# Waits for landed rows ahead of two of the five gathers of a batch, in a two-layer graph network kernel

## The chip, the cores and the metric

One NeuronCore of a Trainium2 chip. The metric is the device time of one execution in microseconds (us), as the median of the runs. The engines are TensorE (PE in the profile; PEld is its weight load), VectorE (DVE), ScalarE (ACT), GpSimd (POOL) and SyncE (SP), which only starts transfers here.

## The reference

12,500 nodes with 32 features, 400,000 edges sorted by destination. Two layers, each followed by a residual add and a layer norm:

```python
x = layernorm(x + L0(x, edge_attr_2, weight, root_w, root_b, edge_index))   # spline convolution
x = layernorm(x + L1(x, edge_weight, edge_attr_3, edge_index, w1, b1, w2, b2))
# L0: basis = _basis(pseudo)                        (E, 9)
#     messages = einsum('ek,ei,kio->eo', basis, x[row], weight)
#     out = zeros.at[col].add(messages) / max(degree, 1) + x @ root_w.T + root_b
# L1: R = relu(dist @ w1 + b1) @ w2 + b2            (E, 384)
#     msg = R, spherical harmonics of rel_vec and features[src], contracted per edge to 32 values
#     out = zeros.at[dst].add(msg)
```

Both layers read one node row per edge (`x[row]`, `features[src]`): that is the gather.

## The kernel before

A *unit* is 5 x 128 = 640 edges (`G = 5`), a *batch* is 5 units (`U = 5`), and there are 125 batches (`B`). For each unit GpSimd runs `gather_unit` (L165 to L171): five indirect DMAs, each of which fetches 128 rows, one for each partition, and adds 16 to `rows_landed[u]` when they are there. In layer 0 a row is 32 floats of `x`, in layer 1 it is 96 floats of `table_dram`. Each of the five units of a batch has its own `rows` buffer and its own `rows_landed` semaphore, so GpSimd may be up to five units ahead of VectorE. The indices stand in two buffers, `idx_a` for units 0 to 2 and `idx_b` for units 3 and 4. SyncE reloads `idx_a` when the rows of units 0 to 2 have landed and `idx_b` when those of units 3 and 4 have (L324, L813); after that, in layer 0, it loads the next batch's destinations and edge attributes.

**Layer 0, the first loop (L360 to L365 on GpSimd).** Batch 0 is gathered ahead of the loop; the loop gathers batches 1 to 124. For unit `u` GpSimd waits for `spread_ready`, which VectorE sets when it has multiplied the rows of the same unit of the batch before (L472), and then gathers. VectorE's `build` (L459 to L474) makes a small `basis` in PSUM (L464), a one-hot matrix of the destinations (L467) and `spread` = basis x rows (L472). Before L464 it waits until TensorE has summed the same unit of the batch before (`summed`), since both share buffers that are five units deep. TensorE's `sum_edges` (L588 to L597) multiplies the one-hot matrix by `spread` (L595). Every batch its `fold` (L605) and `weigh` (L614) finish the messages, which VectorE adds into `acc` (L481).

**Layer 1, the second loop (L827 to L834 on GpSimd).** GpSimd waits for `prods_ready[1]`, set by VectorE's `products` (L1006, L1010) five units before, and gathers. TensorE computes `radials` (L894), three tiles and then two, each followed by a drain that signals `radial_ready` (L895). VectorE multiplies them by the gathered rows. TensorE sums over edges (L904) and turns the sum (L913). Here the ring of work buffers is three units deep (`SLOTS = 3`).

The order is the order of the code on every engine; there is no scheduler. The trace names the gathers by the helper's line L169 in both loops.

Of the kernel before, what the change touches and what calls it, by code (L numbers as in the profile page):

```python
# [27 lines left out]
G = 5  # L28
# [11 lines left out]
EPS = 1e-5  # L40
SLOTS = 3
CREDIT = U


SLOT = [u % SLOTS for u in range(U)]
# [13 lines left out]
def done(g, u):  # L59

    return g * U + (u + 1)


def freed(g, u):

    return g * U + (u - AGO[u] + 1 + CREDIT)


def last_round(g, u):

    return g * U + (u - U + 1 + CREDIT)

# [54 lines left out]
def load_passes(eng, keep):  # L127

    return eng.value_load(keep["span_i"][0:1, 0:1], min_val=0, max_val=N - 1) // WINDOW + 1
# [35 lines left out]
def gather_unit(pool, table, idx, rows, width, u, gathers_begun, rows_landed):  # L165

    pool.sem_inc(gathers_begun, 1)
    for j in range(G):
        pool.indirect_dma_start(out=rows[u][:, j, 0:width], out_offset=None, in_=table,  # L169
                                in_offset=bass.IndirectOffsetOnAxis(ap=idx[u // 3][:, u % 3, j:j + 1], axis=0)  # L170
                                ).then_inc(rows_landed[u], 16)  # L171
# [28 lines left out]
def spline_layer(nc, keep, x, src, dst, edge_attr_2, edge_attr_3, weight0, root_w, root_b, spans_dram, table_dram):  # L200
# [13 lines left out]
    with ExitStack() as ctx:  # L214
# [9 lines left out]
        def sem(name):  # L224
            return ctx.enter_context(nc.semaphore(name))
# [36 lines left out]
        x_ps, root_ps = [pair[:, n, :] for n in range(2)], [msg_ps, side_ps]  # L262
        fold_ps = [bank[:, 0:3 * n * WINDOW].rearrange("k (c w) -> k c w", c=3)
                   for bank, (_, n) in zip((pair[:, 0, :], pair[:, 1, :], side_ps), FOLDS)]
        agg_ps = [pair, sums_all]
        window_ps = own_ps[:, 0:WINDOW]
# [10 lines left out]
        rows_landed = [sem(f"l0_rows_landed{n}") for n in range(U)]  # L277
# [67 lines left out]
        @block.gpsimd  # L345
        def _(pool):
            pool.memset(ident[:, :], 0.0).then_inc(ident_made, 1)
            pool.wait_ge(ident_made, 1)
            pool.affine_select(out=ident[:, :], in_=ident[:, :], compare_op=ALU.not_equal, fill=1.0, base=0,
                               pattern=[[-1, P]], channel_multiplier=1).then_inc(ident_made, 1)  # L350
            pool.iota(keep["iota"][:, :], [[1, WINDOW]], base=0, channel_multiplier=0,
                      allow_small_or_imprecise_dtypes=True).then_inc(ident_made, 1)

            for u in range(U):
                if u in (0, 3):
                    pool.wait_ge(idx_landed[u // 3], 16)
                gather_unit(pool, x, idx, rows, C, u, gathers_begun, rows_landed)
            pool.wait_ge(span_ready, 1)
            passes = load_passes(pool, keep)
            with pool.Fori(0, passes * B - 1) as g:  # L360
                for u in range(U):
                    pool.wait_ge(spread_ready, done(g, u))
                    if u in (0, 3):
                        pool.wait_ge(idx_landed[u // 3], g * 16 + 32)
                    gather_unit(pool, x, idx, rows, C, u, gathers_begun, rows_landed)  # L365

        @block.vector
        def _(dve):
# [107 lines left out]
            def add(g, u, offset):  # L476

                dve.wait_ge(msg_ready, g + 2)
                dve.wait_ge(added, g * U + (u + CREDIT))
                at = acc[0:C + 1, bass.ds(offset, WINDOW)]  # L480
                dve.tensor_tensor(at, at, msg_ps[0:C + 1, u * WINDOW:(u + 1) * WINDOW], ALU.add).then_inc(added, 1)  # L481

            dve.sem_inc(summed, CREDIT)
            dve.sem_inc(msg_ready, 1)
            dve.sem_inc(added, CREDIT)
            LAG = 2
# [68 lines left out]
        def _(pe):  # L555
# [42 lines left out]
            def fold(g, k):  # L598
                u0, n = FOLDS[k]
                pe.wait_ge(flat_ready, done(g, u0 + n - 1) + CREDIT)  # L600
                pe.wait_ge(sums_ready, g * KF + (k + 1))
# [127 lines left out]
def tensor_edges(nc, keep, src, table_dram, edge_weight, w1, b1, w2, b2):  # L729
# [9 lines left out]
    with ExitStack() as ctx:  # L739
# [9 lines left out]
        def sem(name):  # L749
            return ctx.enter_context(nc.semaphore(name))  # L750
# [22 lines left out]
        rows_landed = [sem(f"l1_rows_landed{n}") for n in range(U)]  # L773
# [20 lines left out]
        @block.sync  # L794
        def _(sp):
            for h in range(2):
                sp.sem_inc(idx_landed[h], 16)
            for h in range(2):
                load_dist(sp, 0, h)
            sp.dma_start(w2raw[0:HID, :], w2).then_inc(w_landed, 16)  # L800
            sp.dma_start(w2raw[HID:HID + 1, :], b2.rearrange("(o r) -> o r", o=1)).then_inc(w_landed, 16)
            for h in range(2):
                sp.dma_start(w1c[HID * h:HID * (h + 1), :], w1.rearrange("o h -> h o")).then_inc(w_landed, 16)
                sp.dma_start(b1c[HID * h:HID * (h + 1), :], b1.rearrange("(h o) -> h o", o=1)).then_inc(w_landed, 16)
            passes = load_passes(sp, keep)

            with sp.Fori(0, passes) as p:

                def body(i, after):
                    g = p * B + i  # L810
                    for h, (u0, u1) in enumerate(DIST):
                        for u in range(u0, u1):
                            sp.wait_ge(rows_landed[u], (g + 1) * (16 * G))  # L813
                        load_indices(sp, src, idx, idx_landed, h, after)

                with sp.Fori(0, B - 1) as i:
                    body(i, i + 1)
                body(B - 1, 0)
            for h in range(2):
                sp.wait_ge(idx_landed[h], passes * (B * 16) + 16)  # L820
            sp.sem_inc(indices_done, 1)

        @block.gpsimd
        def _(pool):
            pool.sem_inc(prods_ready[1], CREDIT)
            passes = load_passes(pool, keep)
            with pool.Fori(0, passes) as p:  # L827
                with pool.Fori(0, B) as i:
                    g = p * B + i
                    for u in range(U):  # L830
                        pool.wait_ge(prods_ready[1], g * U + (u - U + 1 + CREDIT))
                        if u in (0, 3):
                            pool.wait_ge(idx_landed[u // 3], (g + 1) * 16)
                        gather_unit(pool, table_dram, idx, rows, ROW, u, gathers_begun, rows_landed)  # L834
# [358 lines left out]
```

## Time and profile before

| | us |
|---|---|
| median of 3 runs | 10573.09 (10558.03 to 10587.41) |
| span of the profiled execution | 10807.3 |
| first loop with its start, from the timeline | 0 to 4790 |
| second loop | 4867 to 10737 |

| engine | busy us | share of the span |
|---|---|---|
| PE | 6974.1 | 65% |
| POOL | 5918.5 | 55% |
| DVE | 5904.1 | 55% |
| ACT | 2697.5 | 25% |

The page has no figure for what lies around the span; the profiled execution's own time is known here as its span, 234 us above the median of the runs. A busy share is a mean over two loops that have different limits, so each loop is read by itself. In an idle time, "issue" as releaser says that nothing in the profile ended it, and "remote" that a semaphore of another engine did which the profile can't tie to one instruction.

### The profile page before, as it was taken

The numbers are of one execution on the slowest core, as the hardware profiler recorded it, in microseconds if no ns is written. First come the engines' busy times: TensorE is split into PE (matmuls) and PEld (weight loads), VectorE is DVE, ScalarE is ACT, GpSimd is POOL, SyncE is SP. The second block draws the span as 40 slices with busy tenths as digits, with TensorE's granted clock in tenths as the row PEclk, the third lists the DMA queues.
The fourth block names the chain that finished last, engine by engine and source line by source line (L and its number), as shares of the span: only waits on it lengthen the run. The fifth ranks groups of instructions, "written<-read, shape, count | busy, mean of one in ns | idle before, by whom it ended". The sixth has DMA issues, their size and how long they took to land. (4 is left out here: it accounts for less than half of the span.)

```text
span 10807.3 us, 123454 instructions
## 1 busy us (share of the span) xinstructions
PE 6974.1 (65%) x30415; PEld 3523.6 (33%) x30415; DVE 5904.1 (55%) x14948; ACT 2697.5 (25%) x6811; POOL 5918.5 (55%) x6257
## 2 busy tenths in 40 slices
PE   5555555555554555556777777777777777777777
PEld 2222222222222222233333333333333333333334
DVE  4333433333333333346666666666666666666667
ACT  1000000000000000013333333333333333333333
POOL 6666666666666666645545554554554555455553
PEclk7666666666666666668888888888888888888888
DMA  1111111111111111112222222222222222222221
GB/s 27 13 13 13 13 13 13 13 13 13 13 13 13 13 13 13 13 27 46 45 43 43 45 45 43 43 45 43 45 43 44 43 43 45 44 44 43 44 45 42
DMA packets 640189, 331.75 MB, mean 31 GB/s; under 512 B 522098, under 2 KB 572413, under 8 KB 639919
## 3 DMA queue, kind: packets, MB, share of 16 engines
q0 software_dynamic: 200000, 205.20, 10.9%
q10 hardware_dynamic: 20000, 102.42, 3.6%
q1 hardware_dynamic: 420168, 23.91, 2.7%
q8 instruction: 8, 0.13, 0.0%
q14 instruction: 13, 0.10, 0.0%
HBM read 324.65 MB, written 6.40 MB: 31 GB/s over the span
## 5 line engine op out<-in xcount | busy, mean ns | idle before, releaser
L595 PE MATMUL sums_all<-shared 128*64 128x289 f32 x6250 | 2028.7, 500 | 2060.9 <-issue 2038.6
L169 POOL DMA_INDIRECT rows<-table_dram,idx_a x1875 | 1776.4, 947 | 1781.0 <-DVE prods L1010 1184.1
L169 POOL DMA_INDIRECT rows<-in_x,idx_a x1875 | 1774.7, 946 | 1450.6 <-DVE shared L472 910.9
L894 PE MATMUL radial_y<-w2p,hidden 128*128 128x384 f32 x2500 | 1226.5, 623 | 1209.0 <-issue 1176.1
L904 PE MATMUL sums_ps<-prods,hot 128*64 128x272 f32 x12500 | 1711.8, 423 | 256.7 <-issue 251.1
L595 PEld LDWEIGHTS sums_all<-shared 128*64 128x64 f32 x6250 | 878.1, 162 | 2988.8 <-issue 2693.5
L169 POOL DMA_INDIRECT rows<-table_dram,idx_b x1250 | 1184.0, 947 | 1204.9 <-DVE prods L1010 842.9
L464 DVE TENSOR_TENSOR own_ps<-factors 128x45 f32<-128x45 f32 x625 | 133.0, 213 | 2645.9 <-remote 2041.0
L864 ACT ACTIVATE hot<-window,rel_t 128x64 f32<-128x64 f32 x3125 | 813.2, 335 | 2487.4 <-PE sums_ps L904 1578.2
L894 PE MATMUL radial_x<-w2p,hidden 128*128 128x384 f32 x3750 | 1378.7, 504 | 34.7 <-issue 34.7
L169 POOL DMA_INDIRECT rows<-in_x,idx_b x1250 | 1182.6, 946 | 381.2 <-issue 380.9
L904 PEld LDWEIGHTS sums_ps<-prods,hot 128*64 128x64 f32 x12500 | 1007.8, 148 | 1142.9 <-issue 842.9
L682 ACT ACTIVATE flat<-sums_all 64x289 f32<-64x289 f32 x625 | 255.2, 408 | 4317.4 <-remote 3176.2
L894 PEld LDWEIGHTS radial_y<-w2p,hidden 128*128 128x128 f32 x2500 | 516.2, 229 | 1820.4 <-issue 1704.2
L1006 DVE TENSOR_TENSOR prods<-radial_x,rows 128x768 f32<-128x768 f32 x625 | 598.5, 958 | 863.2 <-PEq L895 572.5
L472 DVE TENSOR_TENSOR shared<-own_ps,rows 128x1440 f32<-128x1440 f32 x625 | 1030.0, 1648 | 12.2 <-DVE own_ps L464 10.0
L859 ACT ACTIVATE hidden<-dist_ab,b1c,w1c 64x640 f32<-64x640 f32 x625 | 959.4, 1535 | 8.6 <-issue 2.2
L1010 DVE TENSOR_TENSOR prods<-radial_x,rows 128x384 f32<-128x384 f32 x1875 | 923.0, 548 | 0.0
L894 PEld LDWEIGHTS radial_x<-w2p,hidden 128*128 128x128 f32 x3750 | 661.7, 189 | 425.4 <-issue 37.5
L1034 DVE TENSOR_REDUCE red<-sums_ps 128x16 f32<-128x272 f32 x625 | 273.6, 438 | 729.2 <-remote 565.4
L1010 DVE TENSOR_TENSOR prods<-radial_y,rows 128x384 f32<-128x384 f32 x1250 | 632.2, 547 | 0.0
L1019 DVE TENSOR_REDUCE along<-prods 128x40 f32<-128x640 f32 x625 | 506.8, 811 | 0.1
(149 smaller groups left out, 4735.0 us busy)
## 6 DMA issues: line engine op xcount, KB each, us to landing
dist_ab<-in_edge_weight ACTq DMA_DIRECT2D x125, 480.0 KB
dist_ab<-in_edge_weight ACTq DMA_DIRECT2D x125, 320.0 KB
rows<-in_x,idx_a POOLq DMA_INDIRECT x1875
rows<-table_dram,idx_a POOLq DMA_INDIRECT x1875
rows<-in_x,idx_b POOLq DMA_INDIRECT x1250
rows<-table_dram,idx_b POOLq DMA_INDIRECT x1250
vec_s<-in_edge_attr SPq DMA_DIRECT2D x126, 37.5 KB
idx_a<-in_src SPq DMA_DIRECT2D x251, 7.5 KB
```

The source lines that it names most:

```text
L169: pool.indirect_dma_start(out=rows[u][:, j, 0:width], out_offset=None, in_=table, in_offset=bass.IndirectOffsetOnAxis(ap=idx[u // 3][:, u ...
L472: dve.tensor_tensor(spread[s][:, :, 0:K].rearrange("e t (k c) -> e t k c", c=C), basis[s].unsqueeze(3).to_broadcast([P, G, 9, C]), rows[u] ...
L595: last = pe.matmul(sums_ps[s][:, 0:K + 1], hot[s][:, j, :], spread[s][:, j, :], start=(j == 0), stop=(j == G - 1))
L682: act.activation(flat[u][:, :], sums_ps[u][:, 0:K + 1], ACT.Copy).then_inc(flat_ready, 1)
L859: act.activation(hidden[s][0:HID, :].rearrange("h (j p) -> h j p", p=P), dist[u].rearrange("h (p j) -> h j p", j=G), ACT.Relu, bias=b1c[HI ...
L864: last = act.activation(hot[s][:, j, :], keep["window"][:, :], ACT.Abs, bias=rel_t[:, bass.ds(i * (U * G) + (u * G + j), 1)], scale=-1.0)
L894: pe.matmul(radial[h][:, j, 0:R], hidden[s][:, (j0 + j) * P:(j0 + j + 1) * P], w2p[:, :], start=True, stop=True)
L904: last = pe.matmul(sums_ps[s][k * WINDOW:(k + 1) * WINDOW, 0:HALF], hot[s][:, j, :], prods[s][:, j, MUL + 16 * k:MUL + 16 * (k + 1), :].re ...
L1006: dve.tensor_tensor(prods[s][:, j0:j0 + tiles, 0:16, 0:16], ra, comp[:, :, 0:1, :].to_broadcast([P, tiles, 16, 16]), ALU.mult)
L1010: last = dve.tensor_tensor(prods[s][:, j0 + j, 16:OUTS, 0:16].rearrange("e (u o) i -> e u o i", o=3), rb, comp[:, j, 1:4, :].unsqueeze(1). ...
L1019: dve.tensor_reduce(along[:, :, :], prods[SLOT[u]][:, :, 0:MUL, 0:16], AX_X, ALU.add).then_inc(along_ready, 1)
L1034: dve.tensor_reduce(red[s][:, 0:16], sums_ps[s][:, 0:HALF].rearrange("w (o i) -> w o i", i=I17), AX_X, ALU.add).then_inc(red_ready, 1)
```

## The change

`REST = (1, 3)`. In both loops GpSimd, ahead of the gathers of units 1 and 3, waits until all five gathers of the unit before (0 or 2) of the same batch have landed. Nothing is removed, and no instruction changes its place.

```diff
@@ constants
 CREDIT = U
+REST = (1, 3)
@@ first loop, GpSimd
                 for u in range(U):
                     pool.wait_ge(spread_ready, done(g, u))
+                    if u in REST:
+                        pool.wait_ge(rows_landed[u - 1], g * (16 * G) + 32 * G)
                     if u in (0, 3):
                         pool.wait_ge(idx_landed[u // 3], g * 16 + 32)
@@ second loop, GpSimd
                     for u in range(U):
                         pool.wait_ge(prods_ready[1], g * U + (u - U + 1 + CREDIT))
+                        if u in REST:
+                            pool.wait_ge(rows_landed[u - 1], (g + 1) * (16 * G))
                         if u in (0, 3):
                             pool.wait_ge(idx_landed[u // 3], (g + 1) * 16)
```

GpSimd's instructions in the body of the first loop, units 0 to 4, before:

```order
L169 DMA rows<-in_x,idx_a 128x32 [waits l0_idx_a_landed]
L169 DMA rows<-in_x,idx_a 128x32 x4
L362 REGISTER_ALU
L169 DMA rows<-in_x,idx_a 128x32 [waits spread_ready]
L169 DMA rows<-in_x,idx_a 128x32 x4
L362 REGISTER_ALU
L169 DMA rows<-in_x,idx_a 128x32 [waits spread_ready]
L169 DMA rows<-in_x,idx_a 128x32 x4
L362 REGISTER_ALU
L169 DMA rows<-in_x,idx_b 128x32 [waits spread_ready,l0_idx_b_landed]
```

and now (every line is one lower down):

```order
L170 DMA rows<-in_x,idx_a 128x32 [waits l0_idx_a_landed]
L170 DMA rows<-in_x,idx_a 128x32 x4
L363 REGISTER_ALU
L365 ISA [waits spread_ready]
L170 DMA rows<-in_x,idx_a 128x32 [waits l0_rows_landed0]
L170 DMA rows<-in_x,idx_a 128x32 x4
L363 REGISTER_ALU
L170 DMA rows<-in_x,idx_a 128x32 [waits spread_ready]
L170 DMA rows<-in_x,idx_a 128x32 x4
L363 REGISTER_ALU
L170 DMA rows<-in_x,idx_b 128x32 [waits l0_idx_b_landed,spread_ready,l0_rows_landed2]
```

The first gather of unit 1 waits for `l0_rows_landed0` and the first of unit 3 for `l0_rows_landed2` as well; what stood beside it has become one more small instruction (ISA). The second loop changes in the same way, with `l1_rows_landed0` and `l1_rows_landed2`.

## Rows read from the trace of the kernel before

**Rows 1.** The page, fifth part: two groups (busy, mean ns, idle before, releaser).
```profile
L169 POOL DMA_INDIRECT rows<-in_x,idx_a x1875 | 1774.7, 946 | 1450.6 <-DVE shared L472 910.9
...
L464 DVE TENSOR_TENSOR own_ps<-factors 128x45 f32<-128x45 f32 x625 | 133.0, 213 | 2645.9 <-remote 2041.0
```

**Rows 2.** Busy time in the two loops: us, busy (x instructions), TensorE clock, DMA, GB/s.
```profile
0.00:4790.00 4790.00, 2480.10 (x8841) 1187.46 (x8841) 1844.87 (x4743) 424.49 (x1122) 2957.47 (x3132) 0.68 0.13 14
4867.00:10737.00 5870.00, 4391.97 (x21086) 2260.56 (x21086) 3964.05 (x9956) 2227.65 (x5593) 2960.36 (x3125) 0.88 0.21 44
```

**Rows 3.** Timeline, GpSimd, layer 0: start, us, instruction, [idle before <-releaser].
```profile
2015.35 0.95 POOL L169 DMA_INDIRECT rows<-in_x,idx_a  x1 [0.30 <-issue]
2016.61 0.95 POOL L169 DMA_INDIRECT rows<-in_x,idx_b  x1 [0.30 <-issue]
...
2027.86 0.95 POOL L169 DMA_INDIRECT rows<-in_x,idx_b  x1 [0.30 <-issue]
2036.24 0.95 POOL L169 DMA_INDIRECT rows<-in_x,idx_a  x1 [7.43 <-DVE shared L472]
```

**Rows 4.** Timeline, VectorE, the same batch.
```profile
2006.45 1.65 DVE L472 TENSOR_TENSOR shared<-own_ps,rows 128x1440 f32<-128x1440 f32 x1
...
2012.12 0.45 DVE L439 TENSOR_SCALAR factors<-factors 128x50 f32<-128x50 f32 x1 [0.48 <-DVE factors L438]
2033.16 0.21 DVE L464 TENSOR_TENSOR own_ps<-factors 128x45 f32<-128x45 f32 x1 [20.59 <-remote]
...
2033.69 1.65 DVE L472 TENSOR_TENSOR shared<-own_ps,rows 128x1440 f32<-128x1440 f32 x1
```

**Rows 5.** Timeline, TensorE, the same batch.
```profile
2003.88 4.17 PE L595 MATMUL sums_all<-shared 128*64 128x289 f32 x20
...
2024.00 0.64 PE L595 MATMUL sums_all<-shared 128*64 128x289 f32 x1 [2.85 <-issue]
...
2033.45 6.41 PE L595 MATMUL sums_all<-shared 128*64 128x289 f32 x20
```

**Rows 6.** One tile, the load of idx_a: count, duration, first to last start.
```profile
L162 SPq MOVE idx_a<-in_src x1: 29/29/29, 2017.9 to 2017.9; - x1
```

**Rows 7.** One tile, the load of idx_b.
```profile
L162 SPq MOVE idx_b<-in_src x1: 29/29/29, 2030.3 to 2030.3; - x1
```

**Rows 8.** Timeline, GpSimd, an early batch with two pauses.
```profile
269.69 0.95 POOL L169 DMA_INDIRECT rows<-in_x,idx_b  x1 [0.30 <-issue]
273.09 0.95 POOL L169 DMA_INDIRECT rows<-in_x,idx_a  x1 [2.46 <-DVE shared L472]
```

**Rows 9.** Timeline, VectorE, the same early batch.
```profile
281.36 0.21 DVE L464 TENSOR_TENSOR own_ps<-factors 128x45 f32<-128x45 f32 x1 [8.71 <-remote]
```

**Rows 10.** Timeline, GpSimd, layer 1.
```profile
6369.93 0.94 POOL L169 DMA_INDIRECT rows<-table_dram,idx_a  x1 [0.30 <-issue]
6378.09 0.94 POOL L169 DMA_INDIRECT rows<-table_dram,idx_a  x1 [7.21 <-DVE prods L1010]
...
6386.26 0.95 POOL L169 DMA_INDIRECT rows<-table_dram,idx_a  x1 [2.23 <-DVE prods L1010]
...
6393.11 0.95 POOL L169 DMA_INDIRECT rows<-table_dram,idx_b  x1 [0.89 <-issue]
...
6398.11 0.94 POOL L169 DMA_INDIRECT rows<-table_dram,idx_b  x1 [0.30 <-issue]
```

**Rows 11.** Timeline, TensorE, the same stretch of layer 1.
```profile
6372.57 2.92 PE L894 MATMUL radial_y<-w2p,hidden 128*128 128x384 f32 x4 [6.32 <-issue]
...
6381.04 1.55 PE L894 MATMUL radial_y<-w2p,hidden 128*128 128x384 f32 x4
...
6387.86 1.55 PE L894 MATMUL radial_y<-w2p,hidden 128*128 128x384 f32 x4
...
6400.76 2.92 PE L894 MATMUL radial_y<-w2p,hidden 128*128 128x384 f32 x4 [6.14 <-issue]
```

**Rows 12.** Groups of instructions, TensorE, from 4870 to 10730 us.
```profile
L894 PE MATMUL radial_y<-w2p,hidden 128*128 128x384 f32 x2480 | 1218.8, 624 | 1208.6 <-issue 1176.1
```

## The prediction

> **What bounds the kernel now.** I read the mean times of the two loops first, then the timeline of one batch on GpSimd, VectorE and TensorE, then layer 1 in the same way. The first loop takes 4790 us, the second 5870 us, and in neither is an engine full: in the first GpSimd is busy for 2957 us, TensorE for 2480 us, VectorE for 1845 us [rows 2]. So look for what each waits for.
>
> Layer 0. GpSimd issues a gather every 1.25 us (0.95 busy, 0.30 to the next), 25 in a row without a gap: at 2015.35, across the unit boundary at 2016.61, up to 2027.86; then it is idle for 7.43 us, until VectorE's L472 [rows 3]. A batch is therefore 24 x 1.25 + 0.95 + 7.43 = 38.4 us, and all of those pauses are 910.9 us [rows 1]. VectorE for its part stood idle for 20.59 us, from 2012.57 to 2033.16, ahead of L464, the first instruction of a unit; such waits make up most of 2646 us [rows 1, 4]. L464 waits for TensorE's sum of the same unit one batch earlier. TensorE had done 20 matmuls from 2003.88 to 2008.05, two units, at full pace. After that it crawls: at 2024.00 one matmul after 2.85 us in which the profile shows no releaser; at 2033.45 it is suddenly at full pace again [rows 5]. It is not the arithmetic that is late. While GpSimd gathers without a break, signals and issue of TensorE are held up, and they come through when the gathers have drained: GpSimd's last gather ended at 2028.81, VectorE went on at 2033.16 (4.35 us later). VectorE then does L464 to L472, and GpSimd starts 0.90 us after L472's end (2035.34 to 2036.24) [rows 3, 4]. That is a ring: gathers without a break hold up TensorE, TensorE holds up VectorE, VectorE holds up the next batch's gathers.
>
> Layer 1 shows the same thing more sharply. TensorE stops for 6.32 us and resumes at 6372.57; GpSimd's last gather ended at 6370.87, 1.70 us before. It stops for 6.14 us and resumes at 6400.76; the gather ended at 6399.05, 1.71 us before [rows 10, 11]. Both stops fall on a unit gathered hard behind another: ahead of 6393.11 GpSimd was idle for only 0.89 us, whereas the unit at 6386.26, behind a pause of 2.23 us, stopped nobody [rows 10]. From one stop's end to the next is 28.19 us for three units, where a unit without a stop takes 6.82 us (6381.04 to 6387.86): a stop costs 28.19 - 3 x 6.82 = 7.7 us [rows 11]. In all TensorE loses 1176 us this way [rows 12], some 185 stops of 6.3 us, about three in two batches.
>
> **The change part by part.** It adds waits only. Their price first. The rows of the last gather of unit 2 (issued at 2015.35, ended at 2016.30) had landed by 2017.9, when SyncE, which waits for the same semaphore, went on; those of unit 4 ended at 2028.81 and were there by 2030.3 [rows 3, 6, 7]. So a gather's landing is signalled at most 1.5 to 1.6 us after its end. Behind a signal GpSimd needs 0.90 us to its first gather (above). A rest is 1.5 + 0.9 = 2.4 us of idle GpSimd in place of 0.3, so 2.1 us more. Bounds: below, zero, where GpSimd was idle for over 2.4 us anyway; above, 4.35 us of release plus 0.9, 5.0 us more, if the landing signal were held up as TensorE's are.
>
> Behind the waiting instruction stand, on GpSimd, only the gathers of the same and later units. Unit 1's and 2's rows come 2.1 us later, unit 3's and 4's 4.2 us, and with them SyncE's index and stream loads. VectorE consumes rows a batch after the wait for their buffer, so this is covered as long as it is behind GpSimd.
>
> Layer 0, the benefit. The first rest comes 6.25 us into a batch, at a time (2036.24 - 38.4 + 6.25 = 2004.1 in the batch shown) when TensorE still runs at full pace, and a run is then at most three units (3, 4 and the next 0) instead of five. TensorE's sums reach VectorE in the rest or at the latest in the next one, one batch before they are needed. GpSimd then never waits for VectorE and the loop goes at GpSimd's own pace: 25 x 1.25 + 2 x 2.1 = 35.5 us a batch instead of 38.4. Over the 124 batches of the loop: 911 us of pauses go, 37 us of plain 0.30 us gaps take their place, 248 rests of 2.1 us add 521 us. Net: **-353 us**. What is late next is GpSimd itself, with nothing behind it that could fill in.
>
> The Trainium skill, "DMA: Bandwidth & Descriptors", section "Rules for kernel authors", speaks against the change: issue a DMA early and wait on its semaphore late, so that its fixed cost overlaps. Its section on the anatomy of a gpsimd DMA puts that cost at about 2.0 us, near what the row gives. By that rule alone 498 rests would be an added 1.0 ms with nothing in return; the trace's 911 us of pauses, released by VectorE, is what the rule does not see.
>
> Layer 1. GpSimd's own work with rests is 25 x 1.25 + 3 x 0.6 + 2 x 2.1, about 37 us of a batch of 47, so the rests cost nothing on the path: its rows are needed four units later. They can forbid a stop at units 1 and 3, since the pause before those is then 2.4 us. But a stop forbidden at unit 3 likely moves to unit 4, which is gathered hard behind it. Now a stop comes every three units, sometimes four (185 in 625: 3.4 on average). If only 0, 2 and 4 can be hit, the cycle is 0, 4, 2, 0: steps of four, three and three. That is 3.3 to 3.6 on average, between no gain and 11 stops fewer (-85 us). I take **-50 us**. Bounds: -1170 us if the stops all went and GpSimd's 37.7 us set the pace (125 x 9.4), and +60 us.
>
> Sum: -403 us against the span of 10807 us. The median of the runs is 0.978 of that span, so I take 0.978 x 403 = 394 us from it: 10573 - 394 = **10180 us**.
>
> **Rivals.**
>
> A, slower: the rests are too short to let TensorE's signals through in layer 0. For it: there the release came 4.35 us after the last gather, and a rest is 2.4 us; in an early batch GpSimd paused for 2.46 us, from 270.64 to 273.09, and VectorE still waited until 281.36, that is until 2.3 us after the next pause began [rows 8, 9]. Against it: those followed runs of 20 to 25 gathers, while in layer 1 runs of ten released within 1.7 us, and the first rest follows five. If it holds, the pause of 7.4 us stays and 4.2 us are added to each batch: +521 us, 0.978 x 521 = 510, **11083 us**. It decides from the point at which the release needs more than 2.4 us after runs of 10 to 15 gathers. Chance 0.17, half of it a mild form near 10700.
>
> B, much faster: in layer 1 the rests break the pattern, and half of the stops or more are gone. For it: the stops follow short pauses, and two of the five are made long. Against it: GpSimd then lags and gathers units 2, 4 and 0 back to back. Half of 185 stops at 7.7 us is 712 us more: **about 9480 us**; a quarter gives 9830. Chance 0.13.
>
> C, a part: in layer 0 a pause of about 3 us remains at the end of most batches, because the run of units 3, 4 and 0 lasts 18.75 us and holds up VectorE's unit 0. That takes 3 x 124 = 372 us back: **about 10545 us**. Chance 0.12.
>
> D, the waits do nothing: they are met whenever GpSimd reaches them. The gathers at 2015.35 and 2016.61 are 0.30 us apart and the rows of the first came over 1 us later [rows 3, 6], so in layer 0 this can't be. By the skill's rule, same page, section "Issuing engines are not separate DMA queues", transfers of all engines interleave on the same 16 DMA engines. That rule gives a rest nothing to free, and its result is that of A.
>
> **How the numbers follow.** Forecast 0.58, A 0.17, B 0.13, C 0.12. The forecast's own range is 10080 to 10300: the release time of a rest between 1.9 and 2.7 us is 60 us either way, layer 1 another 50. For 8 in 10 the range reaches into C and A's mild form above and into B's weak form below: 9950 to 10620. A measurement of this kernel tells a change from none at about 0.3%, 32 us. Faster: the forecast, B and most of C, less a little for what I haven't seen, 0.77. Same: the edge of C, 0.05. Slower: A and a rest, 0.18.
>
> **What would show it.** In the changed profile the gather at the start of units 1 and 3 of layer 0 has about 2.4 us of idle time ahead of it, released by a DMA, and the one of unit 0 has 0.3 us in place of 7.4. The idle time released by L472 falls from 911 us to near zero, VectorE's waits of 20 us ahead of L464 are gone, and it waits for landed rows ahead of L472 instead. TensorE's crawl no longer fills half of a batch. GpSimd's batch takes 35.5 us in layer 0, and in layer 1 about 46.7 us, with the stops of TensorE on units 0, 2 and 4 alone. The prediction is wrong if the pause of 7 us is still there beside the rests (A), if the rest's idle time is well over 2.4 us, or if layer 1's 1176 us fall by hundreds.

## The result and the profile after

The changed kernel takes **10590.14 us** (median of 20 runs, 10566.73 to 10615.96), the kernel before in the same comparison 10570.44 us (20 runs, 10551.22 to 10592.28): ratio 1.002, 95% interval 1.0012 to 1.0029. I had forecast 10180. The change is no gain but a loss of 0.2%, small and clear of noise. In the traces alone it looks otherwise: the span went from 10807.3 to 10614.2 us.

Busy time in the two loops of the changed kernel, with the columns of [rows 2]:

```profile
0.00:4664.00 4664.00, 2689.24 (x8850) 1259.03 (x8851) 1856.22 (x4746) 421.07 (x1124) 2950.26 (x3132) 0.68 0.12 14
4738.00:10535.00 5797.00, 4336.20 (x21058) 2231.06 (x21058) 3962.17 (x9945) 2232.74 (x5593) 2952.71 (x3125) 0.88 0.20 44
```

Layer 0 is 126 us shorter than in the trace of before, layer 1 is 73 us shorter. What GpSimd and VectorE waited for in layer 0 of the changed kernel, from 100 to 4600 us (in total, times, longest), first GpSimd:

```profile
POOL rows L170 <- issue: 1157.6, 2849, 2.8
POOL rows L170 <- DVE shared L475: 332.4, 72, 6.2
POOL rows L170 <- DMA rows<-in_x,idx_a: 166.9, 94, 2.3
```

and VectorE:

```profile
DVE own_ps L467 <- remote: 1614.6, 192, 19.2
DVE own_ps L467 <- PE sums_all L598: 335.3, 77, 12.2
DVE shared L475 <- DMA rows<-in_x,idx_b: 197.5, 47, 6.1
```

GpSimd's pauses until VectorE fell from 911 us [rows 1] to 341 over the whole loop (332 in the stretch above) and did not vanish. VectorE still stands ahead of L467 (L464 before) for 1615 us, in more and shorter waits; in the same stretch of the kernel before it was:

```profile
DVE own_ps L464 <- remote: 1917.4, 116, 21.7
```

GpSimd's timeline shows the new rests, here ahead of units 1 and 3 (for most of them the profile names no releaser but "issue"), and between them a pause that should be gone:

```profile
2436.52 0.94 POOL L170 DMA_INDIRECT rows<-in_x,idx_a  x1 [2.25 <-issue]
...
2447.44 0.94 POOL L170 DMA_INDIRECT rows<-in_x,idx_a  x1 [4.98 <-DVE shared L475]
...
2455.52 0.95 POOL L170 DMA_INDIRECT rows<-in_x,idx_b  x1 [2.15 <-issue]
```

VectorE in the same stretch:

```profile
2444.43 0.21 DVE L467 TENSOR_TENSOR own_ps<-factors 128x45 f32<-128x45 f32 x1 [16.38 <-remote]
...
2505.09 0.21 DVE L467 TENSOR_TENSOR own_ps<-factors 128x45 f32<-128x45 f32 x1 [13.00 <-remote]
```

The rest from 2434.27 to 2436.52 lies inside VectorE's wait from 2428.05 to 2444.43: the gathers had drained, GpSimd stood still for 2.25 us, and VectorE did not go on. The early batch of before [rows 8, 9] points the same way, more weakly than I read it: VectorE's wait there began at 272.65 (281.36 - 8.71), only 0.44 us before that pause ended. Over the whole loop VectorE stood in a wait of over 1 us ahead of L467 when a rest began in 136 of the 248 rests; in 51 of these its wait ended within the rest, in 20 within 1 us after it, in 65 later.

In layer 1 TensorE's stops are still there:

```profile
L899 PE MATMUL radial_y<-w2p,hidden 128*128 128x384 f32 x2480 | 1213.5, 622 | 1251.5 <-issue 1216.7
```

1217 us where it was 1176 [rows 12]. Counted from the starts of gathers and matmuls, there are 183 stops over 4 us, against 185. By the unit that GpSimd was gathering they fall on units 0 to 4 as 59, 11, 47, 0 and 66 times; before it was 51, 34, 30, 51 and 19.

### The profile page after: what moved, and what is told of

Same layout as the page of the kernel before. It is cut to its first block and busy times, and to the rows that moved or that the text cites. A ratio compares the mean times of both kernels' runs of the same rounds, so it can differ in the third digit from the quotient of the medians.

```text
span 10614.2 us, 123952 instructions
## 1 busy us (share of the span) xinstructions
PE 7132.9 (67%) x30415; PEld 3568.2 (34%) x30415; DVE 5917.6 (56%) x14948; ACT 2699.8 (25%) x6811; POOL 5903.3 (56%) x6257
## 2 busy tenths in 40 slices
DMA packets 640188, 331.75 MB, mean 31 GB/s; under 512 B 522097, under 2 KB 572412, under 8 KB 639918
## 5 line engine op out<-in xcount | busy, mean ns | idle before, releaser
L909 PE MATMUL sums_ps<-prods,hot 128*64 128x272 f32 x12500 | 1666.5, 415 | 193.4 <-issue 187.4
L467 DVE TENSOR_TENSOR own_ps<-factors 128x45 f32<-128x45 f32 x625 | 133.0, 213 | 2173.2 <-remote 1647.9
L909 PEld LDWEIGHTS sums_ps<-prods,hot 128*64 128x64 f32 x12500 | 983.0, 145 | 1057.6 <-issue 737.5
L617 PE MATMUL msg_ps<-sums,wk 96*33 96x320 f32 x750 | 357.9, 637 | 837.3 <-ACT sums L692 430.4
```

Of the source, the lines that this page charges most:

```text
L617: last = pe.matmul(msg_ps[0:C + 1, 0:U * WINDOW], wk[0:m, c, :], sums[0:m, c, :], start=(c == 0), stop=(c == 2))
L909: last = pe.matmul(sums_ps[s][k * WINDOW:(k + 1) * WINDOW, 0:HALF], hot[s][:, j, :], prods[s][:, j, MUL + 16 * k:MUL + 16 * (k + 1), :].re ...
```

## The experiments

All runs of this section, five jobs on five chips, found TensorE never held up, which I learned from the first of them. Each kernel is timed against the kernel before on the same chip.

**The kernel before, unchanged.** No edit.

> The kernel before, unchanged, profiled once more and timed against itself. Question: the traced execution of before took 10807 us, its other 20 between 10551 and 10592; was the trace typical? Theory R (the trace was not typical): the new span is near 10570, and the missing 235 us are in layer 0, where the batch is then about 36.5 us and not 38.4. Theory P (the trace was typical and the chips differ): a span near 10800 beside runs near 10570. Ratio 1.000 in both.

Measured: 8274.84 us (11 runs, 8273.65 to 8276.21), beside 8274.59; ratio 1.000, interval 0.9991 to 1.0009. Neither theory of mine foresaw this. The same program is 2296 us shorter than in the first comparison. Its trace, the two loops and then two groups of the page:

```profile
0.00:3915.00 3915.00, 2453.23 (x8923) 1236.21 (x8924) 1893.48 (x4761) 430.76 (x1136) 2952.29 (x3132) 0.76 0.15 17
3972.00:8203.00 4231.00, 3994.47 (x21087) 2111.06 (x21088) 3883.38 (x9958) 2243.94 (x5595) 2955.45 (x3125) 1.00 0.29 61
```

```profile
L472 DVE TENSOR_TENSOR shared<-own_ps,rows 128x1440 f32<-128x1440 f32 x625 | 1035.1, 1656 | 1598.3 <-DMA rows<-in_x,idx_b 1017.0
...
L169 POOL DMA_INDIRECT rows<-in_x,idx_a x1875 | 1771.8, 945 | 581.0 <-issue 541.1
```

GpSimd gathers in layer 0 without a pause, 31.2 us a batch (25 x 1.25), and VectorE waits for landed rows ahead of L472 (1598 us), no longer ahead of L464 for TensorE. A gather lasts 945 ns, as before (946). In layer 1 a batch takes 33.9 us where it took 47.1, TensorE has no stop over 4 us inside the loop, and its granted clock is 1.00 (2.4 GHz throughout) instead of a mean of 0.88. So the work and the gathers are the same, and what is gone is the holding up of TensorE.

**Rests in one layer at a time, and ahead of four units.** One of the two added waits is left out; in the third run `REST = (1, 2, 3, 4)`.

```diff
 # rests in layer 0 alone (second loop)
-                        if u in REST:
-                            pool.wait_ge(rows_landed[u - 1], (g + 1) * (16 * G))
 # rests in layer 1 alone (first loop)
-                    if u in REST:
-                        pool.wait_ge(rows_landed[u - 1], g * (16 * G) + 32 * G)
```

> Rests in layer 0 alone. Theory R (the ring is real, but the kernel before normally loses less in layer 0 than its trace showed): the same as before within 0.5%, 10520 to 10620 us, with layer 0 at 37.3 us a batch as in the changed kernel. Rival A (a rest only adds its 2.1 us): 248 rests less the pauses they cover, over 10700. My prediction's own sum: 10230.

> Rests in layer 1 alone. The prediction's step: TensorE's stops move to units 0, 2 and 4, their number stays at about 185, and the time changes by 0 to -85 us: 10490 to 10575. If the rests cost time in layer 1: 10600 and more. Together with the run with rests in layer 0 alone this should add up to the changed kernel's +20 us.

> Rests ahead of units 1, 2, 3 and 4 in both layers: the longest run is two units (4 and 0). GpSimd's own pace in layer 0 is then 25 x 1.25 + 4 x 1.95 = 39.1 us a batch. Theory R: in layer 0 no pauses beside the rests remain, since signals get through after each unit, so 39.1 us; in layer 1 GpSimd's own 39 us is under the batch of 46.5 us, and if short runs stop TensorE less often, the stops fall well below 185 and layer 1 gains up to 1000 us. Rival A: pauses of 7 us remain in layer 0 beside the rests (over 44 us a batch) and the stops in layer 1 stay at 180.

Measured, each against 8274.59: layer 0 alone 8745.33 us (ratio 1.0568, interval 1.0553 to 1.0582); layer 1 alone 8506.13 (1.0277, 1.0263 to 1.0291); four rests in both 9997.81 (1.2083, 1.2066 to 1.2099). Theory R and my step for layer 1 could not be tried, because their condition was absent in all three, and their times were missed; rival A's pure price is what is left. Layer 0: 471 us for 248 rests, **1.90 us a rest**, and 35.0 us a batch. With four rests it is 38.8 us a batch, again 1.9 each; theory R's 39.1 for it is met for another reason, as that is GpSimd's own pace. So the price that I worked out of the trace, 2.1 us, was right to 0.2. Layer 1: 231 us for 250 rests, since with rests GpSimd needs 35.9 us a batch and so overtakes VectorE's 33.9 as the limit.

**The changed kernel, and one rest a batch** (`REST = (3,)`).

> The changed kernel itself, timed again beside the kernel before. In the last runs TensorE was nowhere held up: the kernel before took 8275 us and rests in layer 0 and in layer 1 cost 471 and 231 us. Theory H (there are two conditions, with and without held-up signals, whatever the kernel; the change's price is the same in both and its gain is there in one only): where the kernel before takes about 8275 us, the changed one takes 8275 + 471 + 231 = 8977 us; where it takes about 10570 us, the changed one takes 10570 to 10620 us. Rival N (the change is neutral, and the first comparison is what holds in general): the same as before within 0.5% in both.

> One rest a batch, ahead of unit 3 alone, in both layers. Without held-up signals, theory H: half of the price in layer 0 (+235 us) and in layer 1 near nothing to +60 us, since GpSimd's own pace with one rest is 31.3 + 1.9 + a few tenths, just under or over VectorE's 34.0 us a batch: 8510 to 8570 us. With held-up signals: GpSimd's pace in layer 0 is 33.2 us and its run of four units (3, 4, 0, 1, 2 without a break is five) holds TensorE up for most of it, so a pause of about 5 us remains and the time is that of the changed kernel within 1%.

Measured: changed kernel 8997.79 us (1.0872, 1.0857 to 1.0886), one rest 8515.98 (1.0291, 1.0277 to 1.0305). The sum of the parts, 8977, is met to 21 us. Theory H holds and N falls: the near neutrality of the first comparison is no property of the change. The half of H for the held-up condition was not met again, so it rests on the first comparison alone. One rest costs 240 us, all of it in layer 0 (4153 us where it was 3915), and nothing in layer 1 (33.9 us a batch). The changed kernel's loops and what released GpSimd:

```profile
0.00:4389.00 4389.00, 2626.30 (x8928) 1298.16 (x8928) 1881.28 (x4761) 431.69 (x1138) 2949.49 (x3132) 0.72 0.14 15
4447.00:8940.00 4493.00, 4012.44 (x21164) 2118.93 (x21164) 3904.31 (x9995) 2275.61 (x5626) 2969.16 (x3125) 1.00 0.27 58
```

In layer 1 VectorE now waits for rows, which it did not before:

```profile
6003.19 0.28 DVE L986 TENSOR_TENSOR dots<-rows,rho 128x120 f32<-128x120 f32 x1 [1.55 <-DMA rows<-table_dram,idx_a]
...
6018.29 0.28 DVE L986 TENSOR_TENSOR dots<-rows,rho 128x120 f32<-128x120 f32 x1 [1.98 <-DMA rows<-table_dram,idx_b]
```

**A wait that is already met.**

```diff
-REST = (1, 3)
+REST = (3,)
 # both loops, against the changed kernel; in the second the count is (g + 1) * (16 * G)
-                        pool.wait_ge(rows_landed[u - 1], g * (16 * G) + 32 * G)
+                        pool.wait_ge(rows_landed[u - 2], g * (16 * G) + 32 * G)
```

> One wait a batch ahead of unit 3, as in the run before, but for the rows of unit 1, which landed about 5 us earlier, and not for those of unit 2. Theory W (a rest costs what the landing of the last gather and GpSimd's new start take, the wait instruction itself nothing): within 0.1% of the kernel before, where the rest for unit 2's rows cost 241 us. Rival I (a second semaphore wait ahead of a gather costs GpSimd its head start on the descriptors, whether it is met or not): GpSimd's idle time ahead of unit 3 is over 0.3 us by as much as it costs a restart, 0.9 us, and the time is 0.6 x 124 = 75 to 110 us longer.

Measured: 8276.12 us beside 8276.08, ratio 1.000 (0.9991 to 1.0009). W holds, I falls: a wait that is already met costs nothing in the time, and GpSimd's idle time ahead of unit 3 in layer 0 stays at 0.30 us. The price of a rest is the landing plus GpSimd's new start.

**The changed kernel once more.**

> The changed kernel once more, with the kernel before beside it, to see whether the condition in which TensorE is held up returns. If the kernel before takes about 8275 us: the changed one 8990 us. If it takes about 10570 us: the changed one 10570 to 10620 us.

Measured: 8957.34 us beside 8276.08, ratio 1.0822 (1.0805 to 1.0838). The held-up condition did not return, here or later.

**The ring made by hand.** On TensorE, ahead of the sum of unit 0 in layer 0:

```diff
+                        if u == 0 and not last:
+                            pe.wait_ge(rows_landed[4], g * (16 * G) + 32 * G)
 # in the run with the rests of layer 0: rows_landed[2] in its place
```

> The ring of the prediction, made by hand on a chip where nothing holds TensorE up: in layer 0 TensorE waits, ahead of the sum of unit 0 of a batch, until the gathers of the next batch (in flight) have all landed. The results stay the same. Ring theory: GpSimd must pause at the end of each batch for the landing (1.4 us), TensorE's sum (2.1 to 2.6), VectorE's L464 to L472 (2.2) and its own start (0.9), 6.8 us, as in the trace of before (7.1 to 7.4): layer 0 at 37.7 us a batch, total 8275 + 124 x 6.5 = 9080 us. If other slack covers it (VectorE two units ahead, five buffers), the time stays near 8275.

> The same hold, but with the rests of layer 0 and released at the rest ahead of unit 3 (TensorE waits for the rows of unit 2 of the next batch). Ring theory, and my prediction's step for layer 0: no pause is left beside the rests, 35.0 us a batch, 8745 us as with the rests alone, that is 335 us less than with the hold and without rests. If the release in the middle of a batch is too late all the same, a pause remains and the time is between 8800 and 9500.

Measured: hold 9441.85 us (1.141, 1.1391 to 1.1429); hold and rests 8753.35 (1.0578, 1.056 to 1.0596). Where TensorE is held until the gathers have landed, the rest of the ring follows: VectorE waits for TensorE, GpSimd for VectorE, and a batch of layer 0 takes 40.5 us. The link from the gathers to TensorE is put in by hand here, so this says nothing of what makes it in the first comparison. GpSimd's pause is longer than I had worked out:

```profile
2026.95 0.94 POOL L169 DMA_INDIRECT rows<-in_x,idx_a  x1 [9.67 <-DVE shared L472]
```

The reason is on TensorE and VectorE: released at 2018.80, the first sum reached VectorE 5.1 us later and not after 2.1 to 2.6.

```profile
2018.80 6.54 PE L595 MATMUL sums_all<-shared 128*64 128x289 f32 x20 [24.03 <-DMA rows<-in_x,idx_b]
```

```profile
2023.88 0.22 DVE L464 TENSOR_TENSOR own_ps<-factors 128x45 f32<-128x45 f32 x1 [23.52 <-PE sums_all L595]
```

The busy times of that stretch and of the one after it (the clock stands behind GpSimd's):

```profile
2018.80:2023.90 5.10, 5.10 (x15) 2.65 (x16) 0.02 (x1) 0.00 (x0) 0.00 (x0) 0.52 0.28 16
2025.90:2032.90 7.00, 7.00 (x35) 3.99 (x34) 5.07 (x11) 1.52 (x4) 4.72 (x5) 1.00 0.07 9
```

After 24 us of waiting TensorE had a granted clock of 0.52, its lower level, and 7 us later 1.00. With the release at the landing of unit 2's rows, which is also when the rest ahead of unit 3 ends, no pause is left (35.0 us a batch), and the time is that of the rests alone (8753 beside 8745 us). So a release in the middle of each batch is early enough for GpSimd to keep its own pace. It is 688 us less than with the first hold, but two things differ between the runs, the rests and what the hold waits for, and a hold until unit 2's rows without rests was not run: that the rests save these 688 us is not shown. What fails in the first comparison is that a rest often does not bring the release.

**Four gathers instead of five.** Leaves out the fifth gather of each unit in layer 0; its rows are set to zero once, and VectorE and SyncE wait for four gathers.

```diff
-    for j in range(G):
+    for j in range(n):
 # n = G - 1 in layer 0, whose rows_landed counts by 64 instead of 80
```

> Leaves out the fifth gather of each unit in layer 0 (those rows are zero, so an edge in five contributes nothing but its root term); layer 1 is unchanged. Is GpSimd's pace of gathers what layer 0 costs where TensorE is not held up? Theory G: 20 x 1.25 = 25.0 us a batch instead of 31.2, 8275 - 124 x 6.2 = 7500 us. If VectorE or TensorE is close behind as the limit: between 7600 and 8275.

Measured: 7501.35 us (0.9065, 0.905 to 0.908), 774 us less, to 1 us what theory G gives. Where TensorE is free, layer 0 costs what GpSimd takes to issue gathers, 1.25 us each, and nothing else. A rest there can only add.

## Why the prediction was wrong

**What held.** The price of a rest: 2.1 us forecast, 1.90 by timing, and in the changed kernel's trace a median idle time of 2.20 us ahead of units 1 and 3 of layer 0 in place of 0.30. Of the ring in layer 0 the links from TensorE to VectorE and from VectorE to GpSimd, by the run with the hold. In layer 1 the stops moved to units 0, 2 and 4, but for 11 on unit 1, and nearly kept their number (183 for 185).

**What was near by luck.** For layer 1 I took -50 us, as 6 or 7 stops fewer at 7.7 us, and the traces have -73. Two stops fewer are some 15 us, and TensorE's idle time ahead of those matmuls went up, from 1176 to 1217 us. The -73 us came from somewhere else, and since the trace of before is itself 234 us above its runs, they may not be in the runs at all.

**First failure: the base.** I wrote "The median of the runs is 0.978 of that span" and scaled by it. The traced execution, 10807 us, lies 215 us above the longest of 20 runs (10592). That was a sign that the trace held more of something than the runs do, and it need not spread evenly. The traces, compared with each other, give -193 us; the runs give +20. The change's own traced execution (10614.2) is within its runs, though it is the longest of the 20. So of the -403 us that I summed, 193 are seen between the traces and none between the runs. Where the 234 us of the trace of before sit can't be shown, as no other trace of it in that condition exists. That they sat in the pauses that I counted as gain is a guess and not shown. The forecast missed by 410 us. About half of it lies between my sum and what the traces show (the second failure, less what layer 1 gave by luck). The other half lies between the traces and the runs, and its cause stays open.

**Second failure: the release, the step of the mechanism that failed.** The step was "TensorE's sums reach VectorE in the rest or at the latest in the next one", and from it "GpSimd then never waits for VectorE". Of 911 us of pauses 341 stayed, and a batch of layer 0 took 37.3 us, not 35.5 (38.4 before): -126 us between the traces in place of -353. Of VectorE's 225 waits over 2 us ahead of L467 in the changed trace, 134 ended more than 3 us after the last pause of GpSimd had begun, and of the 136 rests that began while VectorE waited 85 brought no release before they ended. A rest of 2.2 us is often too short. Rival A named this mechanism and its evidence [rows 8, 9]; its price was too high since the pause shrinks as the rests come, and I gave its mild form too little.

**Third failure: what I took for the kernel.** This one did not make the forecast miss, since the comparison that it was for ran in the same condition as the trace; it is the largest for anyone who would use the change. "While GpSimd gathers without a break, signals and issue of TensorE are held up" described a condition of that comparison, not the program. In five later jobs, each on another chip, the kernel before took 8274.6 to 8276.1 us (medians), without any hold-up, and the change costs 8.2 to 8.7%. None of my rivals had the other sign for this reason: layer 0 at GpSimd's own pace already, with rests as pure price. The Trainium skill's rule that I quoted and set aside ("DMA: Bandwidth & Descriptors", "Rules for kernel authors", wait late) is what holds there: 1.9 us a rest.

Two small sums were off and change no verdict. A rest's idle time of 1.9 to 2.7 us in place of 2.4 is 124 us one way and 74 the other over 248 rests, not 60. GpSimd's own work in layer 1 adds up to 37.3 us, not the 37.7 used for the far bound, which is then about -1230 us.

**What stays open.** What the hold-up is. Two facts stand beside each other. The held-up traces of the kernel before and of the changed one carry 43,289 and 46,714 records of semaphore updates, the free ones of the same two programs 136,386 and 136,906; and only the held-up ones have waits that read "remote" [rows 1]. And TensorE recovers after gathers stop (1.7 us after the last gather in layer 1; in layer 0 VectorE went on 4.35 us after it [rows 3, 4, 10, 11]). Whether the path that records events holds the engine up and loses records, or something else does both, no run here shows. The Trainium skill, "NOTIFIC — Programmer's Manual", section "When the ring fills", says that a record queue that is full, by its setting, loses the new record, overwrites the oldest or blocks the engine that writes. The first two would fit the missing records and the last one the held-up engine; no run here tries them. The changed kernel's runs of the first comparison and all later ones have a span and a granted clock beside their time, so no time without any recording is there to compare with. Which chip the first comparison ran on isn't known either, so a condition of that chip is as open. Two other causes find nothing in the traces: the held-up trace of before moved the same data as the free one (640,189 and 640,188 packets, 331.75 MB each), and the two queues that load instructions moved 21 packets in one and 20 in the other. Untried for want of the condition are also longer rests and the two layers apart in it.

## What to carry to other kernels

Before you build a sum on a trace, put its span beside the runs: if it lies outside their range, the difference is itself a term, and the waits that the change removes are where it may sit. An engine that is late with "issue" as its only releaser, without a longer instruction anywhere, is a condition to reproduce on a second chip before it is designed around. A wait for a transfer that was just issued costs its landing and the restart every time its engine sets the pace; one for a transfer that had landed cost nothing here.

## What the runs showed of the hardware

- The same program took 10570 us in one comparison and 8275 us in five others, with gathers of 0.946 us in both. The excess was in waits for TensorE, at a mean granted clock of 0.79 against 0.88.
- An indirect DMA of 128 rows costs GpSimd 1.25 us from start to start (0.945 busy, 0.30 between), for rows of 128 bytes and of 384 bytes alike. Leaving out one in five in layer 0 shortened the kernel by 774 us for 625 gathers, 1.24 us each.
- In layer 0 a wait for the gather just issued costs GpSimd 1.9 us: 2.2 us from the last gather's end to the next one's start, in place of 0.3.
- After 24 us of idle TensorE ran its first sum at a granted clock of 0.52 (1.2 GHz, with the rise at its end): 5.1 us from its start until VectorE could go on, where later in the same batch ten passes take 2.65 us at 1.00 (2.4 GHz).
